# Two output banks lent to gate and up in the first feed-forward group, the token-feature chain on other steps, and the second half of z stored and loaded one quad later

## What is computed

```python
x = x + _layernorm(_L0_attn_ref(_layernorm(x), Wq, Wk, Wv, Wo))
x = x + _layernorm(_L0_ffn_ref(_layernorm(x), gate_cp, up_cp, down_cp))
# _L0_ffn_ref: gate = h @ gate_w.T ; up = h @ up_w.T      (512 -> 2048)
#              inter = silu(gate) * up ; return inter @ down_w.T
```

## Time and profile before

| | us |
|---|---|
| median of 3 runs | 756.93 (756.38 to 761.38) |
| the profiled execution | 758.16, of which 756.4 are the span |
| PE busy | 676.6 (89%) |
| DVE busy | 512.7 (68%) |
| POOL busy | 430.7 (57%) |
| ACT busy | 365.5 (48%) |
| first matmul of the feed-forward block | at 389.7 |
| mean granted clock of PE | 0.955 of full speed |

### The profile page before, as it was taken

How to read it: one execution, slowest core, us unless ns; L and a number is a source line. 1 busy time by engine, 2 the same in 40 slices (tenths; PEclk the granted TensorE clock), 3 DMA queues, 4 the chain that set the end, 5 groups by cost and what they waited for, 6 DMA issues and landing times. The chain is left out here.

```text
span 756.4 us, 16316 instructions
## 1 busy us (share of the span) xinstructions
PE 676.6 (89%) x5872; PEld 476.1 (63%) x5872; DVE 512.7 (68%) x993; ACT 365.5 (48%) x635; POOL 430.7 (57%) x615
## 2 busy tenths in 40 slices
PE   5996799999999999989947699898989899898996
PEld 3685686878687887867723255565655566564565
DVE  7666773588646973575656668887878878774653
ACT  3532232333232432333335677776777677574641
POOL 5269858547681958910425556564656546554642
PEclk9899899999999999999967899999999999998999
DMA  6814547324561447411786827567394946548123
GB/s 228 309 56 156 182 169 249 119 77 144 190 217 59 159 159 250 138 53 25 209 219 188 186 66 178 131 178 172 123 191 134 206 120 183 123 120 183 63 71 98
DMA packets 65549, 114.98 MB, mean 152 GB/s; under 512 B 12624, under 2 KB 29136, under 8 KB 65488
## 3 DMA queue, kind: packets, MB, share of 16 engines
q1 hardware_dynamic: 65488, 114.16, 52.4%
HBM read 81.76 MB, written 32.37 MB: 151 GB/s over the span
## 5 line engine op out<-in xcount | busy, mean ns | idle before, releaser
L1328 POOL TENSOR_TENSOR act<-inter,act 128x512 f16<-128x512 f32 x128 | 149.6, 1169 | 135.1 <-ACT act L1369 135.0
L1373 ACT ACTIVATE gated<-gbank,c_gate 128x512 f32<-128x512 f32 x128 | 88.0, 687 | 104.0 <-PE gbank L1542 104.0
L1442 DVE SCALAR_TENSOR_TENSOR inter<-ubank,c_up,gated 128x512 f32<-128x512 f32 x128 | 95.6, 747 | 49.8 <-ACT gated L1373 47.8
L1583 PE MATMUL ybank<-down,act 128*128 128x160 f16 x512 | 112.2, 238 | 0.0
L1584 PE MATMUL ybank<-down,act 128*128 128x160 f16 x512 | 111.5, 237 | 0.0
L1585 PE MATMUL ybank<-down,act 128*128 128x160 f16 x512 | 111.4, 236 | 0.0
L1369 ACT CAST act<-inter 128x512 f16<-128x512 f32 x128 | 78.2, 611 | 1.7 <-DVE inter L1442 1.7
L1583 PEld LDWEIGHTS ybank<-down,act 128*128 128x128 f16 x512 | 50.7, 99 | 39.2 <-issue 35.4
L1542 PE MATMUL gbank<-z,s_all 128*32 128x512 f16 x512 | 53.3, 407 | 24.3 <-DMA z<-token_features 15.9
L1542 PE MATMUL ubank<-z,s_all 128*32 128x512 f16 x512 | 52.7, 402 | 8.3 <-DVE inter L1442 7.5
L1584 PEld LDWEIGHTS ybank<-down,act 128*128 128x128 f16 x512 | 51.0, 100 | 3.8
(11 more groups left out here) (195 smaller groups left out, 1943.5 us busy)
## 6 DMA issues: line engine op xcount, KB each, us to landing
x_ln<-x SPq DMA_DIRECT2D x64, 256.0 KB, 3.5
z<-token_features SPq DMA_DIRECT2D x64, 256.0 KB, 5.9
job<-job_in SPq DMA_DIRECT2D x24, 640.0 KB, 4.3
shared<-x SPq DMA_DIRECT2D x32, 256.0 KB, 2.7
x<-shared SPq DMA_DIRECT2D x32, 256.0 KB, 2.0
token_features<-z_hi SPq DMA_DIRECT2D x32, 256.0 KB, 4.2
x_res<-x SPq DMA_DIRECT2D x32, 256.0 KB, 2.7
out<-x_res SPq DMA_DIRECT2D x32, 256.0 KB, 2.1
```

Of the source, the lines that this page charges most:

```text
L1328: pool.tensor_tensor(hidden[par][:, i, TOK:2 * TOK], inter[:, i % INTERS, :], hidden[par][:, i, 0:TOK], ALU.subtract).then_inc(inter_ready, 1)
L1373: act.activation(gated[:, slot % 2, :], gbank[:], ACT.Silu, scale=c_gate[:]).then_inc(silu_done, 1)
L1442: dve.scalar_tensor_tensor(out=inter[:, i % INTERS, :], in0=ubank[:], scalar=c_up[:], in1=gated[:, i % 2, :], op0=ALU.mult, op1=ALU.mult). ...
L1583: pe.matmul(out, hidden[par][:, r, high], box[:, 0], start=False, stop=False)
```

## The change

The diff goes through SP, ACT, DVE and PE in this order. Three edits are made together. In steps 0 to 15 of the first group odd steps write gate and up into the two `ybank` banks, so that gate waits for the silu two steps before, and up for the product two steps before (`pair_of`). The feature chain stands on other steps in every group. And `regroup` is cut in two: half 0 is stored and loaded at the end of the second quad, half 1 at the end of the third.

```diff
+        def pair_of(n):
+            return ybank if isinstance(n, int) and n < I and n % 2 else (gbank, ubank)
...
-            def regroup(g, par, loads_before):
-                for half in range(2):
-                    sp.wait_ge(z_loaded[1 - par][half], loads_before * 64)
-                    feats.spill(sp, half, g, 1 - par)
-                for half in range(2):
-                    ffn_in.load_z(sp, feats, g, par, half)
+            def regroup(g, par, half, loads_before):
+                sp.wait_ge(z_loaded[1 - par][half], loads_before * 64)
+                feats.spill(sp, half, g, 1 - par)
+                ffn_in.load_z(sp, feats, g, par, half)
...
-                if j == 1 and not (isinstance(g, int) and g == GROUPS - 1):
-                    regroup(g + 1, 1 - par, count)
+                if j in (1, 2) and not (isinstance(g, int) and g == GROUPS - 1):
+                    regroup(g + 1, 1 - par, j - 1, count)
...
+                if isinstance(n, int) and 2 <= n < I:
+                    act.wait_ge(inter_done, n - 1)
-                act.activation(gated[:, slot % 2, :], gbank[:], ACT.Silu, ...
+                act.activation(gated[:, slot % 2, :], pair_of(n)[0][:], ACT.Silu, ...
...
-                    if s == 0 and made:
-                        feats.high(act, g * Q + j + AHEAD)
+                    if s == 3 and begun:
+                        feats.high(act, g * Q + j + AHEAD + 1)
                     if s == 3 and made:
                         feats.z_high(...)
...
-                    if s == 2 and made:
-                        feats.turn_copy(dve, m, z_banks)
                     if not (isinstance(n, int) and n >= STEPS - 2):
                         product(n + 2, i + 2)
+                    if s == 1 and made:
+                        feats.turn_copy(dve, m, z_banks)
...
-                    if s == 0 and made:
-                        feats.low(dve, m)
-                    if s == 1 and begun:
+                    if s == 0 and begun:
                         feats.stats(dve, m + 1, (j + AHEAD + 1) % RING, loads)
+                    if s == 2 and begun:
+                        feats.norm(dve, m + 1, (j + 1 + AHEAD) % RING)
                     if s == 3 and made:
                         feats.z_low(...)
                     if s == 3 and begun:
-                        feats.norm(dve, m + 1, (j + 1 + AHEAD) % RING)
+                        feats.low(dve, m + 1)
...
+                first = isinstance(n, int) and n < I
+                gate, up = pair_of(n)
-                    if not (isinstance(n, int) and n == 0):
+                    if not first:
                         pe.wait_ge(free, n)
+                    elif n >= 2:
+                        pe.wait_ge(free, n - 1)
...
-                    if s == 1 and made:
+                    if s == 0 and made:
                         feats.turn(pe, m, z_banks, id16)
                     if s == 2 and made:
                         feats.products(pe, m, z_banks)
```

More of the change, by code:

```diff
@@ L1372, in silu_at @@
                 act.wait_ge(gate_done, n + 1)
-                act.activation(gated[:, slot % 2, :], gbank[:], ACT.Silu, scale=c_gate[:]).then_inc(silu_done, 1)
+                if isinstance(n, int) and 2 <= n < I:
+                    act.wait_ge(inter_done, n - 1)
+                act.activation(gated[:, slot % 2, :], pair_of(n)[0][:], ACT.Silu, scale=c_gate[:]).then_inc(silu_done, 1)
             def moment_hi(g, bank):
@@ L1423, in _ @@
             feats.z_high(act, Q + 1, 1, 1, z_banks)
+            feats.high(act, Q + 2)
             schedule(act, quad)
@@ L1441, in product @@
                     dve.wait_ge(inter_ready, n - INTERS + 1)
-                dve.scalar_tensor_tensor(out=inter[:, i % INTERS, :], in0=ubank[:], scalar=c_up[:],
+                dve.scalar_tensor_tensor(out=inter[:, i % INTERS, :], in0=pair_of(n)[1][:], scalar=c_up[:],
                                          in1=gated[:, i % 2, :], op0=ALU.mult, op1=ALU.mult).then_inc(inter_done, 1)
@@ L1514, in _ @@
             feats.norm(dve, Q + 2, 2)
+            feats.low(dve, Q + 2)
             schedule(dve, quad)
@@ L1536, in gate_up @@
                 side, c = i // HALF, i % HALF
-                for w, bank, free, done in ((GATE, gbank, silu_done, gate_done), (UP, ubank, inter_done, up_done)):
-                    if not (isinstance(n, int) and n == 0):
+                first = isinstance(n, int) and n < I
+                gate, up = pair_of(n)
+                for w, bank, free, done in ((GATE, gate, silu_done, gate_done), (UP, up, inter_done, up_done)):
+                    if not first:
                         pe.wait_ge(free, n)
+                    elif n >= 2:
+                        pe.wait_ge(free, n - 1)
                     for u in range(4):
```

## The result

The changed kernel takes 762.21 us (median of 20 runs, 758.16 to 764.83), the kernel before 758.59 beside it (20 runs, 751.66 to 763.58). The ratio is 1.006, 95% interval 1.0038 to 1.0082. Forecast was a gain of 13 us; there is a loss of some 4. The profiled execution took 763.64 us, of which 761.9 are the span.

A forecast was written before the change was run, and what follows sets the result against it. PE's work and its waits bound the later groups; -7.2 (groups 2 to 5), -1.1 (group 1), -3.1 (group 6) and -1.6 (first group) sum to -13.0: 744 us against the runs, own range 736 to 752.

The forecast's parts named there:

- Half 0 of z ahead of half 1: Group borders: half 0's transfer takes 13 us instead of 15.0; PE's z waits go, 1.2 us left in group 6.
- The loop on DVE: Later groups' feature chain, norm to next norm: 9.26 us without x_res, 10.0 with it; a group takes 41.25 against 43.06.
- What x_res takes: Residual addition on DVE: 0.75 us, being 0.11 us ahead of POOL's next remainder; 1.68 as the other end.
- Rival one: Later groups: POOL goes first at x_res, some 20 quads take 0.93 us more, 762 against the median; chance 0.25.
- The first group: New ring about as long as the old, 0; with the z wait at its end and the first transposes, -1.6 us.
- Rival two: First group: two pairs of banks take the product's and gates' waits from the steps, some 9 us: 735; chance 0.10.

The follow-up runs named there:

- The cut remainder: The changed kernel with POOL's remainder in groups 2 to 5 made on 16 of 512 columns, order and waits kept: 749.18 us, ratio 0.9873.

## Why the prediction was wrong

**Half 0 of z ahead of half 1** held, but for the last border. The z waits went from seven to one, no stretch at the low clock follows the borders from 475 to 653 us, and the split alone is worth 11 to 15 us. The transfer takes 13 us, as estimated. In the last border it leaves 2.78, forecast 1.2, and a low-clock stretch that was forecast to go; groups 6 and 7 gained 1.0 and not 3.1.

**The loop on DVE** held but for one step. Its terms from norm to norm in the quad shown: norm to the product 1.31 (forecast 0.45); product of s = 3 to that of s = 1 4.82 (513.01 + 1.31 to 519.14; forecast 5.31 - 0.45 = 4.86); to o_stats 1.27 by the copy's 0.67 and 0.60 (1.24); o_stats to x_res 2.69 (2.71); x_res to the norm 0.66 (0.75). Together 10.75, forecast 10.0, and the first term alone is 0.86 longer; the others together are 0.12 shorter. PE's wait at up, forecast about 0.5, is 0.80.

**What x_res takes** was chosen rightly: 0.75, by a lead of 0.11 on paper and 0.11 to 0.12 in the traces. It was not luck: in the quad shown both follow from POOL's first factor at 510.64, x_res 1.71 and the remainder 1.83 behind it (512.35 and 512.47), where the forecast had 1.71 and 1.82, and the lead is 0.12 in all 20 such quads. **The step that failed is the one behind it:** "After norm comes the product of s = 3, +0.45 (510.55 to 511.00)". That row is of a norm with no POOL beside it. I let x_res win the race against POOL's remainder and followed x_res alone. The remainder that lost did not go away: it ran directly behind x_res, where the change had put the norm, and the norm waited for it. I had even forecast the remainder "at 1.5 and more", which meets the next instruction of DVE, and did not ask what that was. The cut remainder shows it: same order, norm at 0.54, quads as forecast.

The Trainium skill (SBUF — State Buffer, Who interferes with whom) lists `tensor_scalar`, which the norm is, among the DVE operations that can take the ports shared with GpSimd, when their operands meet the conditions of a two-port mode; whoever issues first then has them for the whole instruction, and the other blocks. I weighed this section for x_res, an operation with two SBUF inputs, and not for the norm with one. The traces agree, with 1.39 against 0.54 for the norm; that it ran in such a mode no row shows by itself. The other figure, 0.71 against 0.21 for POOL's short remainder, is beside x_res, the operation with two inputs.

**Rival one** (POOL first at x_res, 762 us) came to the measured time with the wrong instruction: x_res is 0.75, and the same loss fell on its neighbour. Its price per quad was 0.93, that of the norm is 0.79 over the four quads of a middle group (44.41 less 41.25, by 4). Some 20 such quads make 15.8, and 744 + 15.8 = 759.8, close to the 762.2 measured.

**The first group** (-1.6 with the start of the next) is not wrong in the way that the tally says. At a like clock (0.75 against 0.74) the new order with the banks is 1.6 to 2.1 shorter than the kernel before, and the profiled execution of the changed kernel fell on 0.62; over the whole span it has the lowest clock of the 20 runs (0.956, the others 0.959 to 0.972). That the order or the banks made it shorter is not shown, since the split alone has 40.93 at 0.79. Rival two, 6 to 9 us from the banks, is out: with the banks alone the group is 0.9 shorter, and none of the three first groups with the new order and the banks is more than 2.2 below the kernel before.

What stays open is what sends one and the same first group to 0.62 or to 0.75.

**Even with the norm at its old price the order costs.** The quads with the short remainder sum to 41.3 a group; the split and the banks with the old order have 9.86 to 9.90 three times and 10.7 to 10.8, 40.3 to 40.4 without z waits. The forecast's gain was the split's, less 1 us a group for the chain; the norm took 3 more.

## What to carry over

When two engines take turns on something, follow both of them past the meeting: the one that loses is late, and stands beside whatever the winner's engine does next. Before an order is changed, write down for each instruction of the new order what the other engine does at that moment, and take its price from a row with the same neighbour. And try the parts of a change alone: here one part was worth 11 to 15 us and another took it back.

## What was not expected of the hardware

The norm, one SBUF tensor in and one out, takes 0.54 us by itself and 1.38 beside POOL's remainder, in 15 of 15 cases between 480 and 640 us; a lag of 0.12 us of POOL behind x_res settles which of three instructions wait, in every quad alike. And 16 columns on POOL took 0.71 us in place of 0.21, when it came 0.11 us behind a DVE instruction that has two SBUF inputs.
